# Row maxima, shifts and strips of the second attention's first two units, found inside the last three blocks of the projection ahead of it

## The reference, cut to what matters

```python
q, k, v = proj(Wq), proj(Wk), proj(Wv)                 # 16 heads, 32 wide
scores = (q_r @ k_r.T + q_i @ k_i.T) / sqrt(16)
probs = softmax(where(causal, scores, -inf))
s = concat(probs @ v) @ Wo
g = x @ w_int4 + bias + (x @ a) @ b
```

## Time and profile before

| | us |
|---|---|
| median of 3 runs | 3025.88 (3023.87 to 3026.47) |
| profiled execution, its own time | 3017.3 |
| its span on the core | 3015.5 |
| mean granted clock of TensorE | 0.964 |

### The profile page before, as it was taken

The page is one execution under the profiler, slowest core; times in us unless marked ns, Lnnn a source line. Parts: engine busy times, 40 slices in busy tenths (PEclk is TensorE's granted clock), DMA queues, the critical chain, the costliest instruction groups (busy, mean ns, idle before and its releaser), DMA issues. The chain is left out here.

```text
span 3015.5 us, 46320 instructions
## 1 busy us (share of the span) xinstructions
PE 2836.4 (94%) x18017; PEld 1315.2 (44%) x18017; DVE 2016.5 (67%) x4387; ACT 1540.1 (51%) x2565; POOL 985.5 (33%) x529
## 2 busy tenths in 40 slices
PE   7998999999999973999999999899999999999999
PEld 4664333333333342676666645323333333333327
DVE  7887889999999844000001765688887877878823
ACT  3552467776767764222221444345565565566571
POOL 1000000110111103121100430157777777777791
PEclk9997799999999996999999999789999999999999
DMA  4322121233213124222110466212020220202103
GB/s 130 96 77 76 34 49 35 48 62 62 48 26 62 27 58 139 65 74 87 60 49 28 149 189 193 74 35 62 9 64 12 67 64 8 64 12 67 67 12 119
DMA packets 140923, 200.57 MB, mean 67 GB/s; under 512 B 14320, under 2 KB 107520, under 8 KB 137616
## 3 DMA queue, kind: packets, MB, share of 16 engines
q1 hardware_dynamic: 130288, 173.00, 20.7%
q0 software_dynamic: 9056, 24.59, 3.9%
q10 hardware_dynamic: 1360, 0.01, 0.0%
HBM read 121.01 MB, written 76.02 MB: 65 GB/s over the span
## 5 line engine op out<-in xcount | busy, mean ns | idle before, releaser
L940 ACT ACTIVATE at_probs<-at_st 128x512 f32<-128x512 f32 (+3 forms) x1280 | 588.4, 542 | 442.5 <-PE at_st L1034 283.8
L903 POOL TENSOR_TENSOR at_probs<-at_probs 128x2048 f32<-128x2048 f32 (+3 forms) x205 | 725.9, 3546 | 214.3 <-ACT at_probs L940 135.8
L387 DVE TENSOR_REDUCE at_part<-at_s 128x1 f32<-128x512 f32 (+3 forms) x1280 | 689.3, 601 | 68.5 <-PE at_s L425 33.0
L362 ACT ACTIVATE at_probs<-at_st 128x1024 f32<-128x1024 f32 (+3 forms) x640 | 541.8, 895 | 279.9 <-PE at_st L444 144.4
L966 DVE TENSOR_REDUCE at_part<-at_s 128x1 f32<-128x512 f32 x768 | 498.3, 682 | 68.8 <-PE at_s L1026 65.0
L960 DVE CUSTOM_DVE_ANT_0 at_s<-at_s,at_later 128x384 f32<-128x384 f32 (+3 forms) x512 | 246.6, 497 | 103.9 <-PE at_s L1026 102.6
L504 PE MATMUL at_acc<-at_probs,at_v 128*32 128x512 f32 (+3 forms) x2560 | 308.3, 556 | 8.1 <-ACT at_otile L349 7.8
L2319 DVE TENSOR_TENSOR ex_ot<-ex_bank,lin_b 128x512 f32<-128x512 f32 x32 | 22.1, 692 | 439.1 <-PE ex_bank L2349 439.1
L1858 POOL DMA_DIRECT2D att_sums<-att x28 | 14.7, 529 | 757.0 <-DMA att<-at_otile 757.0
L2292 ACT ACTIVATE ex_hT<-ex_bank,ex_b 128x512 f32<-128x512 f32 x128 | 87.9, 687 | 334.5 <-PE ex_bank L2339 334.5
L2339 PE MATMUL ex_bank<-ex_xT,lin_w 128*128 128x512 f32 x512 | 225.2, 598 | 1.0 <-ACT ex_xT L2285 1.0
(11 more groups left out here) (340 smaller groups left out, 3941.9 us busy)
## 6 DMA issues: line engine op xcount, KB each, us to landing
att<-at_otile SPq DMA_DIRECT2D x64, 256.0 KB, 2.1
lin_w<-in_W SPq DMA_DIRECT2D x16, 1024.0 KB, 7.7
at_v<-v SPq DMA_DIRECT2D x11, 1024.0 KB, 11.9
v<-pr_vt SPq DMA_DIRECT2D x32, 256.0 KB
exp_out<-ex_ot SPq DMA_DIRECT2D x32, 256.0 KB, 2.1
v<-p_vt SPq DMA_DIRECT2D x32, 256.0 KB, 3.7
p_xs<-in_x SPq DMA_DIRECT2D x8, 512.0 KB, 5.0
qhi<-p_parts SPq DMA_DIRECT2D x8, 512.0 KB, 3.3
```

The costliest lines, as they stand in the source:

```text
L362: act.activation(probs[:, quad % RING, heads_down * p:heads_down * (p + 1), off:QB], st_ps[n % st_slots][:, :, off:QB], ACT.Exp, scale=EXP ...
L387: dve.tensor_reduce(part[:, w % 2, qt * HG + h, j:j + 1], s_ps[n % S_SLOTS][:, 0:width], AX.X, ALU.max).then_inc(item_free, 1)
L903: pool.tensor_tensor(total, total, probs[:, slots.slot[quad], :, off:QB], ALU.add).then_inc(add_done, 1)
L940: act.activation(probs[:, slots.slot[quad], h, off:QB], st_ps[n % ST_SLOTS][:, off:QB], ACT.Exp, scale=EXP_SCALE).then_inc(exp_done, 1)
```

## The change

The first two units of the attention, (0,0) and (0,1), get their first pass in the projection. Their score tiles are put as 24 pairs (two heads to one bank tile) behind named jobs of blocks 5, 6 and 7, by the table `EARLY_SLOTS`; their shifts, transposes (`row 0` behind `qA 6`, `row 1` behind `vB 7`) and strips follow, and SyncE writes both strips into `carried.q`. The pairs and rows are entries of the same list `jobs`, so they take turns in the same ring of three bank tiles. GpSimd makes the mask `later` in the projection too. In the attention the planner starts its list of tiles at unit (0,2), with both strips taken as there; the first `ST` of these units waits for `carried.row_ld` alone. Group 1's loads are issued at the start, not behind the second strip.

```diff
+EARLY = 2
+EARLY_TILES = [(u, qt, h, j) for u in range(EARLY) for qt in range(4) for h in range(0, HG, 2) for j in range(u + 1)]
+EARLY_SLOTS = [(slot, b) for b, slots in ((5, "kB kB vA vA vB vB T y"), (6, "qB qB kB kB vA vA vB vB T y"),
+                                          (7, "qB qB kB kB vA vA")) for slot in slots.split()]
+EARLY_AT = {at: [i for i, other in enumerate(EARLY_SLOTS) if other == at] for at in EARLY_SLOTS}
+EARLY_LAST = [max(i for i, tile in enumerate(EARLY_TILES) if tile[0] == u) for u in range(EARLY)]
+EARLY_TURN = {("qA", 6): 0, ("vB", 7): 1}
...
-    for unit in units:
+    for unit in units[EARLY:]:
...
-    exp_end, pv_end, row_at, add_end, sum_end = [], [], {}, [], []
+    exp_end, pv_end, row_at, add_end, sum_end = [], [], {unit: 0.0 for unit in units[:EARLY]}, [], []
...
             for h in range(HG):
                 sp.dma_start(KT[1][K:K + 2, h, :], C["shift_rows"][2 * h:2 * h + 2, h, :]).then_inc(const_ld, 16)
+            load(sp, 1)
...
-                    sp.wait_ge(strip_ready, w + 1)
+                    sp.wait_ge(strip_ready, w - EARLY + 1)
                     for h in range(HG):
                         sp.dma_start(QT[g % 2][K:K + 2, h, u * QB:(u + 1) * QB],
                                      strip[2 * h:2 * h + 2, w % 2, :]).then_inc(row_ready[w % 2], 16)
-                    if w == 1:
-                        load(sp, 1)
...
+            dve.wait_ge(later_ready, 1)
             dve.memset(nothing[:, :], 0.0).then_inc(nothing_ready, 1)
...
-                        pe.wait_ge(row_ready[place_of[ev[1]] % 2], 16 * HG * (place_of[ev[1]] // 2 + 1))
+                        if place_of[ev[1]] < EARLY:
+                            pe.wait_ge(carried.row_ld, 16 * HG * EARLY)
+                        else:
+                            pe.wait_ge(row_ready[place_of[ev[1]] % 2], 16 * HG * (place_of[ev[1]] // 2))
...
+    def early_jobs(at):
+        for i in EARLY_AT.get(at, ()):
+            pe_names.append(f"S {i}")
+            jobs.append((f"S {i}", "dve", f"max {i}"))
+        if at in EARLY_TURN:
+            u = EARLY_TURN[at]
+            pe_names.append(f"row {u}")
+            jobs.append((f"row {u}", "dve", f"strip {u}"))
+
     for b in range(NB):
         for s in ("qA", "qB", "kA", "kB"):
             pe_names.append(f"{s} {b}")
             jobs.append((f"{s} {b}", "dve", f"lo {s} {b}"))
+            early_jobs((s, b))
...
-            dve_names += [f"lo qA {b}", f"lo qB {b}"]
+            dve_names += [f"lo qA {b}"] + early_names("qA", b) + [f"lo qB {b}"] + early_names("qB", b)
...
-        dve_names += [f"lo kB {b}", f"y {b}"]
+        dve_names += [f"lo kB {b}"]
+        for s in ("kB", "vA", "vB", "T"):
+            dve_names += early_names(s, b)
+        dve_names += [f"y {b}"] + early_names("y", b)
...
+                for u in range(EARLY):
+                    if b == NB - EARLY + u:
+                        dve_s.wait(sp, f"strip {u}")
+                        for h in range(HG):
+                            sp.dma_start(carried.q[96:98, h, u * QB:(u + 1) * QB], strip[2 * h:2 * h + 2, u, :]
+                                         ).then_inc(carried.row_ld, 16)
             sp.wait_ge(part_out, 64 * NB)
             sp.wait_ge(v_kept, 64 * NB)
+            sp.wait_ge(carried.row_ld, 16 * HG * EARLY)
...
+            pool.memset(later[:, :], 0.0).then_inc(cleared, 1)
+            pool.wait_ge(cleared, 1)
+            pool.affine_select(out=later[:, QB - P:QB], in_=later[:, QB - P:QB], compare_op=ALU.is_ge, fill=MASK,
+                               base=0, pattern=[[-1, P]], channel_multiplier=1).then_inc(later_ready, 1)
...
+            def maxima(i):
+                u, qt, h, j = EARLY_TILES[i]
+                width = QB if j < u else (qt + 1) * P
+                pe_s.wait(dve, f"S {i}")
+                tile, row = banks.tile(f"S {i}"), qt * HG + h
+                if i == 0:
+                    dve.wait_ge(later_ready, 1)
+                if j < u:
+                    last = dve.tensor_reduce(part[:, u, row:row + 2, j:j + 1], tile[:, :, 0:width], AX.X, ALU.max)
+                else:
+                    for y in range(2):
+                        last = dve.tensor_tensor_reduce(out=tile[:, y, 0:width], in0=tile[:, y, 0:width],
+                                                        in1=later[:, QB - width:QB], scale=1.0, scalar=MASK,
+                                                        op0=ALU.add, op1=ALU.max,
+                                                        accum_out=part[:, u, row + y, j:j + 1])
+                step(f"max {i}", last)
+
+            def shifts(u):
+                dve_s.wait(dve, f"max {EARLY_LAST[u]}")
+                link(dve.tensor_reduce(rowmax[:, u, :], part[:, u, :, 0:u + 1], AX.X, ALU.max))
+                link(dve.tensor_scalar(shift[:, u, :, 0], rowmax[:, u, :], -1.0 / MSHIFT, None, ALU.mult))
+                step(f"shift {u}", stt(out=shift[:, u, :, 1], in0=rowmax[:, u, :], scalar=-1.0 / MSHIFT,
+                                       in1=shift[:, u, :, 0], op0=ALU.mult, op1=ALU.subtract))
+
+            def early(s, b):
+                for i in EARLY_AT.get((s, b), ()):
+                    maxima(i)
+                    if i in EARLY_LAST:
+                        shifts(EARLY_LAST.index(i))
+                if (s, b) in EARLY_TURN:
+                    u = EARLY_TURN[s, b]
+                    pe_s.wait(dve, f"row {u}")
+                    step(f"strip {u}", dve.tensor_copy(strip[:, u, :],
+                                                       banks.tile(f"row {u}")[0:2 * HG, 0, 0:QB // 2].bitcast(F16)))
...
                 lower(1, "k", "B", b)
+                for s in ("kB", "vA", "vB", "T"):
+                    early(s, b)
...
+            def early(s, b):
+                for i in EARLY_AT.get((s, b), ()):
+                    u, qt, h, j = EARLY_TILES[i]
+                    width = QB if j < u else (qt + 1) * P
+                    d = banks.take(pe, f"S {i}")
+                    if i == 0:
+                        pe.wait_ge(carried.group_ld, Carried.GROUP_LOADS)
+                    for y in range(2):
+                        mm = pe.matmul(d[:, y, 0:width], carried.q[0:96, h + y, u * QB + qt * P:u * QB + (qt + 1) * P],
+                                       carried.k[0:96, h + y, j * QB:j * QB + width], start=True, stop=True)
+                    step(f"S {i}", mm)
+                if (s, b) in EARLY_TURN:
+                    u = EARLY_TURN[s, b]
+                    dve_s.wait(pe, f"shift {u}")
+                    d = banks.take(pe, f"row {u}")[0:2 * HG, 0, 0:QB // 2].bitcast(F16)
+                    for qt in range(4):
+                        mm = pe.transpose(d[:, qt * P:(qt + 1) * P], shift[:, u, qt * HG:(qt + 1) * HG, :]
+                                          .rearrange("p h two -> p (h two)"), C["ident_f16"][:, :])
+                    step(f"row {u}", mm)
```

More of the change, by code:

```diff
@@ L727, in __init__ @@
         self.v = c.sb("v", [P, NKC, HG * 32], F32)
-        self.group_ld, self.w_ld = c.sem("group_ld"), c.sem("w_ld")
+        self.group_ld, self.w_ld, self.row_ld = c.sem("group_ld"), c.sem("w_ld"), c.sem("row_ld")
         self.a_ld = [c.sem(f"a_ld{k}") for k in range(NB // B)]
@@ L957, in _ @@
                     if j == u:
-                        if n == 0:
-                            dve.wait_ge(later_ready, 1)
                         dve.tensor_tensor_reduce(out=s_ps[n % S_SLOTS][:, 0:width], in0=s_ps[n % S_SLOTS][:, 0:width],
@@ L986, in _ @@
                     dve.wait_ge(item_ready, n + 1)
-                    if t >= 2:
-                        dve.wait_ge(row_ready[t % 2], 16 * HG * (t // 2))
+                    if t >= EARLY + 2:
+                        dve.wait_ge(row_ready[t % 2], 16 * HG * (t // 2 - 1))
                     dve.tensor_copy(strip[:, t % 2, :], s_ps[n % S_SLOTS][0:2 * HG, 0:QB // 2].bitcast(F16)
                                     ).then_inc(strip_ready, 1)
-                    dve.wait_ge(strip_ready, t + 1)
+                    dve.wait_ge(strip_ready, t - EARLY + 1)
                     dve.nop().then_inc(item_free, 1)
@@ L1058, in _ @@
                     pe.wait_ge(item_free, n - S_SLOTS + 1)
-                    pe.wait_ge(shift_ready, t + 1)
+                    pe.wait_ge(shift_ready, t - EARLY + 1)
                     rows = s_ps[n % S_SLOTS][0:2 * HG, 0:QB // 2].bitcast(F16)
@@ L2399, in combine_and_project @@
             jobs.append((f"{s} {b}", "act", f"{s} {b}"))
+            early_jobs((s, b))
         if b + 1 < NB:
             pe_names.append(f"T {b + 1}")
+            early_jobs(("T", b))
         pe_names.append(f"y {b}")
         jobs.append((f"y {b}", "dve", f"y {b}"))
+        early_jobs(("y", b))
     act_after = {9: ["silu 0"], 12: ["sqrt 0"], 15: ["silu 1"]}
@@ L2428, in combine_and_project, with early_names @@
         dve_names += [f"nrm {m}"] + dve_after.get(m, [])
+    def early_names(s, b):
+        names = []
```

(19 more changed lines are left out.)

## The result

The changed kernel takes 3049.26 us (median of 4 runs, 3043.95 to 3056.05), the kernel before beside it 3024.88 (3020.94 to 3026.47). The ratio is 1.0079, 95% interval 1.0063 to 1.0094: 24 us slower, where 3029 was forecast and 3040 was the end of the range.

A forecast was written before the change was run, and what follows sets the result against it. TensorE, busy 94% of the span, was taken as the bound. Terms of 27 - 28 + 4 = +3 us on the profiled 3017.3 gave 3020, plus 8.6 to the median: 3029 us, range 3019 to 3040.

The forecast's parts named there:

- The projection, +27: Blocks 5 to 7 and hand-over: 23.9 us of matmuls and bank waits, 1.2 hand-over, 2 clock; bounds 24 and 34.
- the hand-over: Projection's end to attention's start: strip DMAs issued behind the values add 0 to 2.4 us, taken as 1.2.
- the walk through the ring: Projection blocks 5 to 7: each job waits for the bank three places ahead; waits of 5.1, 2.1 and under 1 us.
- The walk's shares of work: Added score matmuls and transposes in the projection: 2.4, 3.5 and 2.7 us in blocks 5, 6 and 7; 8.4 counted.
- rival A: Projection's four 2 us gaps also drop the clock, 1.7 us each: projection +34, total 3036; includes (1,2)'s strip costing 9; chance 0.35.
- The attention up to (0,2), -28: Attention's start to the strip copy of unit (0,2): 66.6 us falls to 28.6, taken as 28 less; bounds 24 and 32.
- Both holes: TensorE's waits before the first steps of units (0,0) and (0,1), 14.35 and 11.8 us, would go.
- ScalarE's table load: Attention's opening: the exponential's table load, covered by the first hole before, would now cost 1 us.
- From there on, +4: From (0,2)'s strip copy to unit (2,1): about 7 us lost at (1,2)'s strip, half of 6.5 regained; bounds 0.5 and 9.
- the stall at (1,2)'s shift: Old order's 3.77 us TensorE idle plus half clock, 6.5 us, would be covered by steps; half was counted.
- B: Rival, faster: opening runs at VectorE's pace, saving 32 not 28, and (1,2)'s shift stall vanishes; 3018 to 3021, chance 0.2.
- C: Rival: the attention's first step still waits for the projection's two strips, costing at most 2.4 us; chance 0.02.

The follow-up runs named there:

- two_rings: Changed kernel with the projection's score pairs alternating between the three-bank ring and the transposes' tile, none behind block 5's keys; ratio 1.0024 to the kernel before.
- strip_first: Changed kernel with SyncE issuing group 2's seven loads behind the strip DMAs of unit (1,2), not ahead; ratio 1.0026 to the kernel before.
- before_load_first: Kernel before with group 1's seven loads issued at the attention's start, ahead of the strip of unit (0,0); ratio 1.0030 to the kernel before.
- other_queue: Changed kernel with the four strip DMAs of unit (1,2) issued by ScalarE in its own queue; ratio 1.0042 to the kernel before.
- old_tail: Changed kernel with the order of body from unit (1,2)'s shifts on taken from the kernel before; ratio 0.9994 to the kernel before.

## Why the prediction was wrong

**The projection, +27: right.** Five kernels with that ring have +27.4 to +28.2, and the profiled run of the changed kernel +30.7. To `y` of block 7 it is 26.9 where 23.9 plus 2 for the clock was counted, the hand-over 0.6 where 1.2 was. All waits were where the walk through the ring put them. two_rings shows for blocks 6 and 7 that they are the ring's; with them and block 5's wait gone 10.8 is left. (The walk's shares of work, 2.4, 3.5 and 2.7, add to 8.6 and not to the 8.4 counted before; it changes nothing.)

**The clock in the ring's gaps, rival A: in part.** The prediction held that a gap of 2 us costs nothing, by one trace. In the changed kernel's trace the granted clock fell behind both gaps of 1.98 us in block 6, but not behind those of 1.76 and 1.66 in block 7 (the last of the three rows, 1.00):

```profile
1893.00:1897.00 4.00, 3.03 (x5) 1.33 (x6) 2.56 (x6) 0.00 (x0) 0.00 (x0) 0.80 0.53 183
...
1905.00:1909.00 4.00, 3.68 (x5) 1.65 (x6) 1.91 (x6) 0.00 (x0) 0.00 (x0) 0.57 0.68 239
...
1930.00:1934.00 4.00, 3.21 (x8) 1.54 (x9) 2.91 (x6) 0.00 (x0) 0.00 (x0) 1.00 0.56 197
```

strip_first has the same two gaps, and its clock stays 1.00:

```profile
1865.00:1869.00 4.00, 2.02 (x8) 0.90 (x7) 2.72 (x5) 1.11 (x1) 0.00 (x0) 1.00 0.12 43
...
1877.00:1881.00 4.00, 3.73 (x9) 1.63 (x10) 1.86 (x6) 0.00 (x0) 0.00 (x0) 1.00 0.69 243
```

Blocks 5 to 6, `y` to `y`, take 37.4 us in the first and 34.0 in five others. So rival A's drops exist, cost 3.4 us, and came in one of six traces. The very gap on which the prediction relied, 2.13 us ahead of `y` of block 0, tells the same: in before_load_first the clock fell behind it,

```profile
1729.25 5.41 PE L2792 MATMUL p_bank<-p_w_ffn,p_xT 128*128 128x256 f32 x16 [2.12 <-DVE p_parts L2668]
...
1729.00:1733.00 4.00, 3.75 (x10) 2.98 (x11) 0.19 (x1) 3.08 (x3) 2.37 (x3) 0.57 0.78 257
```

and `y` took 5.41 us there and in other_queue, 3.72 in the eight other traces. One trace was too little to call it free. The 5.1 us gap drops it in all of them (5.40 to 6.32 for a `vA` of 3.70). What decides at 2 us stays open.

**The attention up to (0,2), -28: right.** It is -28.3 in the changed kernel and -28.0 to -28.4 in the five others with the new opening. Both holes went, and 38.2 us were left of 66.6. One of its small terms was not there: ScalarE's table load ran from 1957.27 to 1958.55, and the exponential then still waited 0.62 us for TensorE, so the load cost nothing where 1 us was put.

**From there on, +4: this step failed, and by itself it made the prediction wrong.** The prediction put it as "some 4 us idle, and the clock at 0.50 for a while afterwards", 7 in all, against half of 6.5 avoided. The place was right. The sign of the other half too: the stall at (1,2)'s shift is gone. The idle time was 15.28, and not for VectorE's maxima of the 16 tiles: 15 of these took TensorE from 2094.53 to 2100.77, with a sum among them, while the strip, copied at 2095.88, would have landed by about 2100 (an estimate, from the 3.5 us of the earlier trace rows). It was for the strip's DMA. I walked the moved strip past TensorE's and VectorE's instructions and not past SyncE's, where the event that it was moved behind, (0,3)'s last value matmuls, is the one that issues seven loads. With the loads out of the way (strip_first) the segment is +6.4, near the recorded +4 and inside its bounds of 0.5 and 9, but that nearness is luck: the 4 us idle for VectorE and the half clock behind them did not come, and the old order, which had the stall that was to be avoided, is 9 us better (old_tail, -2.6). What the planner's order costs beyond that strip, the prediction put at nothing. With 21.4 in place of 4 the forecast would have been 3046.

**The rivals.** None had this mechanism. B (the opening at VectorE's pace) did not come. C fell: the first step starts 0.91 us after the first tile.

## What to carry to other kernels

When a step is moved, list for every queue what now stands ahead of it, bulk loads first: a DMA of 8 KB behind 4 MB lands when they do, and here a second queue gave back only half, with the DMA engines 0.97 busy. Small jobs in a ring of banks cost little as single jobs between long ones (0.7 us and less in two_rings). Two together cost 0.3 to 0.7 us here where the next long job waited for a bank of v, 1.7 to 2.0 for one of q or k, and 5.1 where VectorE had other work ahead of reading it; ask which bank the next long job takes. An idle time that the profile gives to "issue" ahead of an instruction that needs a DMA is a reason to read the DMA queue's own rows.

## What was not expected of the hardware

A 2 us gap may or may not halve TensorE's clock: the same gaps of 1.98 us left it at 1.00 in five traces and took it to 0.80 and 0.57 (means over 4 us) in one, and behind a gap of 2.13 us `y` ran slow in two traces of ten. A strip of 8 KB behind 4 MB of loads in one queue took 17.6 us from issue to use, in a queue of its own beside them 11.1, and with no loads ahead of it 3.5.
